# An order of its own for the first head group, and maxima ahead of record turnings in the last tile slot

## What is computed

```python
x = x + attn_a(layernorm(x), w_qkv_a, w_o_a)
x = x + scale * (layernorm(x) @ (2*kernel - 1))
x = x + attn_b(layernorm(x), w_qkv_b, w_o_b)
x = x + scale * (layernorm(x) @ (2*kernel - 1))
# attn: qkv = x @ w_qkv; rope on q and k; four query heads share a key head
# scores = q @ k.T * 0.25, causal; probs = softmax(scores); out = (probs @ v) @ w_o
```

## Time and profile before

| what | value |
|---|---|
| median of 3 runs | 1512.0 us (1511.1 to 1519.8) |
| the profiled execution, its own time | 1511.48 us |
| its span, first to last instruction | 1509.7 us |
| mean granted TensorE clock | 0.949 |

### The profile page before, as it was taken

How to read it: one execution, slowest core, us unless ns; L and a number is a source line. 1 busy time by engine, 2 the same in 40 slices (tenths; PEclk the granted TensorE clock), 3 DMA queues, 4 the chain that set the end, 5 groups by cost and what they waited for, 6 DMA issues and landing times.

```text
span 1509.7 us, 28518 instructions
## 1 busy us (share of the span) xinstructions
PE 1358.1 (90%) x11076; PEld 796.5 (53%) x11076; DVE 1094.9 (73%) x1587; ACT 893.2 (59%) x1704; POOL 384.7 (25%) x591
## 2 busy tenths in 40 slices
PE   5989999999898999999889899999988889999997
PEld 4854444446675444444667544444567744444455
DVE  6667888847767888883776688888376668888647
ACT  3536776773354776775335377777624547777752
POOL 3422222111342222221134222222123412222201
PEclk9988999999897999999999699999999969999999
DMA  3000000001000000000220000000010000000011
GB/s 116 1 1 10 9 16 3 2 2 43 1 1 2 9 16 10 2 3 1 84 70 1 2 9 17 10 2 3 2 41 1 1 1 10 17 9 3 3 51 47
DMA packets 12980, 23.99 MB, mean 16 GB/s; under 512 B 1072, under 2 KB 4144, under 8 KB 12848
## 3 DMA queue, kind: packets, MB, share of 16 engines
q1 hardware_dynamic: 12848, 22.19, 4.3%
HBM read 16.94 MB, written 4.19 MB: 14 GB/s over the span
## 4 chain that ended last, share of the span: by engine, by line
PE 73%; DVE 16%; issue 6%; ACT 3%; POOL 1%; DMA 0%; DVEq 0%; ACTq 0%; POOLq 0%; SPq 0%
PE psO L675 20%; PE psM L539 15%; PE psE L654 14%; PE psM L612 12%; DVE mx L1027 8%; PE psE L592 3%; PE psO L592 3%; PE psM L522 2%; PE psM L619 2%; ACT probs L857 2%; DVE stats L934 1%; PE psM L639 1%; DVE xn L954 1%; DVE attn L1053 1%; PE psE L522 1%
## 5 line engine op out<-in xcount | busy, mean ns | idle before, releaser
L857 ACT ACTIVATE probs<-psE 128x512 f32<-128x512 f32 x1152 | 625.6, 596 | 293.4 <-PE psE L654 287.0
L1027 DVE TENSOR_REDUCE mx<-psM 128x2 f32<-128x768 f32 (+4 forms) x704 | 693.3, 1026 | 121.4 <-PE psM L619 96.3
L612 PE MATMUL psM<-kT,qT 48*128 48x384 f32 (+5 forms) x1536 | 314.5, 423 | 47.4 <-DVE mx L1027 36.6
L675 PE MATMUL psO<-probs,v_grp 128*32 128x512 f32 (+3 forms) x3072 | 324.3, 511 | 0.0
L654 PE MATMUL psE<-qT,kT 50*128 50x512 f32 (+3 forms) x1536 | 293.5, 420 | 15.3 <-ACT probs L857 10.2
L1227 POOL TENSOR_SCALAR_AFFINE_SELECT probs<-probs 128x512 f32<-128x512 f32 x256 | 160.0, 637 | 563.1 <-ACT probs L857 531.0
L612 PEld LDWEIGHTS psM<-kT,qT 48*128 48x128 f32 x1536 | 153.1, 196 | 161.6 <-DVE mx L1027 119.7
L654 PEld LDWEIGHTS psE<-qT,kT 50*128 50x128 f32 x1536 | 134.0, 191 | 171.6 <-ACT probs L857 127.2
L619 PE MATMUL psM<-mask_b 64*128 64x64 bf16 x2048 | 123.9, 201 | 0.0
L675 PEld LDWEIGHTS psO<-probs,v_grp 128*32 128x32 f32 x3072 | 68.4, 110 | 91.1 <-issue 68.5
L539 PE MATMUL psM<-wq_hi,xT_hi 128*128 128x512 f32 (+1 forms) x384 | 98.6, 379 | 9.2 <-ACT vs L823 4.7
(11 more groups left out here) (80 smaller groups left out, 1304.0 us busy)
## 6 DMA issues: line engine op xcount, KB each, us to landing
probs<-in_w_qkv SPq DMA_DIRECT2D x5, 1536.0 KB, 6.5
xs<-in_x SPq DMA_DIRECT2D x8, 512.0 KB, 3.8
xn<-in_w_o SPq DMA_DIRECT2D x16, 256.0 KB, 2.5
out_x<-xs SPq DMA_DIRECT2D x8, 512.0 KB, 2.8
qT<-nm_rows SPq DMA_DIRECT2D x128, 8.0 KB
probs<-in_w_ffn SPq DMA_DIRECT2D x1, 256.0 KB, 8.3
attn<-in_mask SPq DMA_DIRECT2D x1, 160.0 KB, 7.8
sin_s<-in_sin SPq DMA_DIRECT2D x1, 128.0 KB, 8.0
```

Source lines behind the costliest of these rows:

```text
L612: return pe.matmul(psM[:, 2 * pair + h % 2, to:to + k1 - k0], qT[lo:lo + MAXROW, g, qt // QT_PER_CHUNK, h // 2, qt % QT_PER_CHUNK * P:(qt ...
L675: ins = pe.matmul(psO[VW * j:VW * (j + 1), off:off + w], v_grp[:, kb, :], probs[:, (g * NS + s) % PSLOTS, at(j), to:to + w], start=s in (0 ...
L857: act.activation(probs[:, (g * NS + s) % PSLOTS, at(heads[0]):at(heads[0]) + len(heads), 0:w], psE[:, n % SRING, 0:w * len(heads)].rearran ...
L1027: dve.tensor_reduce(to, src, AX.X, ALU.max, negate=True).then_inc(ring_used.sem, 1)
```

## The change

There are three parts. In slot 9, a table of its own puts the two units U.0 and U.1 of tile 6 ahead of the record turnings, and N.0 of group 0 behind R.0 and R.1 (on DVE: behind the copy of R.0). Slot 10 is gone: the units of tile 7 (V.0 to V.3 in the new table) stand in the new `FIRST_ORDER`, the order of group 0 alone, between its first score products. There, Y is `meet(0)`, and the second half of `nm_parts_of(0, ...)` moves on POOL behind the second mask. `FIRST_ORDER` moves N.1.0 and the other entries too. The other groups keep their order. `SLOT_FILL` is not used, and the slices of `cos_s` and `sin_s` are written in another way with the same meaning.

```diff
+FIRST_ORDER = """
+V.0 S.0 V.1 S.1 V.2 S.2 V.3 Y S.3 U.0 PV.0.0 S.4 U.1 PV.1.0 N.1.0 U.2 PV.2.0 OC.0.0 U.3
+S.5 U.4 O.0.0 S.6 U.5 S.7 U.6 U.7 S.8 U.8 PV.3.0 S.9 U.9 U.10 S.10 PV.4.0 U.11 S.11 U.12 S.12 U.13 PV.5.0
...
-PE_SLOT = "TX U.0 Q.0 R.0 R.1 U.1 Q.1 R.2 U.2 R.3 Q.2 R.4 U.3 R.5 Q.3"
...
-SLOTS_A = range(-4, TILES + 4)
-SLOT_NM = TILES + 1
+SLOT_FILL, SLOT_LAST = 2, TILES + 1
+PE_SLOT = {None: "TX U.0 Q.0 R.0 R.1 U.1 Q.1 R.2 U.2 R.3 Q.2 R.4 U.3 R.5 Q.3"}
...
+PE_SLOT[SLOT_LAST] = "U.0 U.1 R.0 R.1 N U.2 R.2 R.3 U.3 R.4 R.5"
+DVE_SLOT[SLOT_LAST] = "U.0 U.1 RC.0 N U.2 RC.3 U.3"
+SLOTS_A = range(-4, TILES + 2)
...
-    return [w for w in words(GROUP_ORDER) if has_prev or len(w) < 3 or w[2] >= 0]
+    return words(GROUP_ORDER if has_prev else FIRST_ORDER)
...
                     for s in DIAGONAL:
                         mask(g, s)
+                        if g == 0 and s == DIAGONAL[1]:
+                            nm_parts_of(0, 1)
...
                 nm_parts_of(0, 0)
-                nm_parts_of(0, 1)
                 group(0, True)
```

More of the change, by code:

```diff
@@ L216 @@
        "RC": 2, "ST": -4, "RS": -3, "AP": -2}
-PE_SLOT = "TX U.0 Q.0 R.0 R.1 U.1 Q.1 R.2 U.2 R.3 Q.2 R.4 U.3 R.5 Q.3"
-ACT_SLOT = "HI RC.1 RC.2 RS PH RC.4 RC.5 QC"
-DVE_SLOT = "AP COS U.0 RC.0 LO ROPE U.1 RC.3 U.2 ST U.3"
-SLOTS_A = range(-4, TILES + 4)
-SLOT_NM = TILES + 1
+SLOT_FILL, SLOT_LAST = 2, TILES + 1
+PE_SLOT = {None: "TX U.0 Q.0 R.0 R.1 U.1 Q.1 R.2 U.2 R.3 Q.2 R.4 U.3 R.5 Q.3"}
+ACT_SLOT = {None: "HI RC.1 RC.2 RS PH RC.4 RC.5 QC"}
+DVE_SLOT = {None: "AP COS U.0 RC.0 LO ROPE U.1 RC.3 U.2 ST U.3"}
+PE_SLOT[SLOT_LAST] = "U.0 U.1 R.0 R.1 N U.2 R.2 R.3 U.3 R.4 R.5"
+DVE_SLOT[SLOT_LAST] = "U.0 U.1 RC.0 N U.2 RC.3 U.3"
+SLOTS_A = range(-4, TILES + 2)
 def slot_work(text, n):
     out = []
-    for what, *arg in words(text):
+    for what, *arg in words(text.get(n, text[None])):
+        if what == "N":
+            out.append((what, arg, 0))
+            continue
         t = n - LAG[what]
@@ L257, in ring_jobs @@
     for n in SLOTS_A:
-        if n == SLOT_NM:
-            out.append((("N", 0, 0), None))
-        out += [(("U", 0, units_of(t)[arg[0]]), unit_pair(units_of(t)[arg[0]])) for what, arg, t in slot_work(PE_SLOT, n) if what == "U"]
+        for what, arg, t in slot_work(PE_SLOT, n):
+            if what == "N":
+                out.append((("N", 0, 0), None))
+            elif what == "U":
+                out.append((("U", 0, units_of(t)[arg[0]]), unit_pair(units_of(t)[arg[0]])))
     turn = 0
@@ L263, in ring_jobs @@
         for what, *arg in group_order(g > 0, g < KV - 1):
-            if what in ("U", "N", "O"):
-                out.append(((what, g + 1, arg[0]) if what == "U" else (what, g + arg[1], arg[0]), turn % 2))
+            if what in ("U", "V", "N", "O"):
+                job = ("U", 0, units_of(TILES - 1)[arg[0]]) if what == "V" else ("U", g + 1, arg[0]) if what == "U" else (what, g + arg[1], arg[0])
+                out.append((job, turn % 2))
                 turn += 1
@@ L732, in group @@
                             tiles[what](arg[0], arg[0] % 2)
+                        elif what == "V":
+                            unit(0, units_of(TILES - 1)[arg[0]])
                         elif what == "U":
@@ L744, in round_ @@
                 for n in SLOTS_A:
-                    if n == SLOT_NM:
-                        nm_turn(0, 0)
                     for what, arg, t in slot_work(PE_SLOT, n):
-                        if what == "TX" and t > 0:
+                        if what == "N":
+                            nm_turn(0, 0)
+                        elif what == "TX" and t > 0:
                             turn_xn(r, t, t % 2)
@@ L882, in group @@
                             o_copy(g + arg[1], arg[0])
-                        else:
+                        elif what not in ("X", "Y", "V", "U", "N"):
                             other(what, arg[0] if arg else None)
@@ L1058, in group @@
                     for what, *arg in group_order(has_prev, has_next):
-                        if what == "U":
+                        if what == "V":
+                            unit(0, units_of(TILES - 1)[arg[0]])
+                        elif what == "U":
                             unit(g + 1, arg[0])
-                        elif what == "X":
-                            meet(g + 1)
+                        elif what in ("X", "Y"):
+                            meet(g + 1 if what == "X" else 0)
                         elif what == "N":
@@ L1068, in round_ @@
                 for n in SLOTS_A:
-                    if n == SLOT_NM:
-                        nm_copy(0, 0)
                     for what, arg, t in slot_work(DVE_SLOT, n):
-                        if what == "LO" and t > 0:
+                        if what == "N":
+                            nm_copy(0, 0)
+                        elif what == "LO" and t > 0:
                             lo(r, t, psE[:, t % 2, :])
@@ L1085, in round_ @@
                             ln_a(r, t)
-                meet(0)
                 group(0, False, True)
@@ L1171, in rope_sin @@
                     t4 = t_s[:, k].rearrange("p (h a d) -> p h a d", a=2, d=HALF)
-                    sn = sin_s[:, bass.ds(l, 1), t, :]
+                    sn = sin_s[:, l:l + 1, t, :]
                     for a in range(2):
```

4 lines of the change are left out of this document (3 added, 1 removed).

## The result

The changed kernel is slower: 1551.41 us, median of 4 executions, beside 1515.9 for the kernel before, ratio 1.020 (95% interval 1.014 to 1.027). 1487 had been forecast. Executions of one and the same kernel scatter here, those of the kernel before from 1509 to 1575 (66 of them, 19 above 1530), and the ratios leave out the ones far above their kernel's fastest. What the scatter is turned out to be half of the answer.

A forecast was written before the change was run, and what follows sets the result against it. TensorE, 90% busy, was taken to set the pace, the changed stretch costing mostly low clock. Gains of 30.6 us from 1511.48 gave 1480.9; 6.0 us of clock falls made 1487, own range 1480 to 1496.

The forecast's parts named there:

- Slot 9: From where TensorE ran dry to V.0: 7.8 us, where it was 11.45 in round 1 and 9.99 in round 2.
- rival two: Clock stays down in group 0 as before, only slot 9 gains 13.1 us: time 1498, chance 0.19.
- The waits up to S.5: Group 0, V.0 at 101.65 to S.5 at 113.0: TensorE idle about 1.7 us for N.1's rows, transfer 2.4.
- sum at full clock: Slot 9 through group 0: 7.8 + 31.35 = 39.1 us per round, gaining 30.6 us in four rounds, so 1480.9.
- 18 maxima, then fully loaded: Group 0 from S.5: VectorE fully loaded with 18 maxima, 17.8 us, 20.0 with copy, division and gaps.
- the clock: Before S.5 the clock may fall: 0.65 per round, 1.5 falls of 1.54 us each, 6.0 us over four rounds.
- the clock stays down as before: Same as rival two: group 0 stays at low clock, only slot 9 gains; 1498, chance 0.19.
- The fall behind S.5: Clock fall from the thin stretch U.2, PV.2, U.3 and 1.7 us idle before S.5; given 0.65 per round.
- what follows S.5 is dense, so I count 1.5 such falls: Group 0 after S.5: dense work limits the cost to 1.5 falls of 1.54 us each time.
- The slower rival: Low clock over the whole stretch from V.0 on, 52.9 us per round: time 1536, chance 0.05.
- The rule on short idle moments: Short idle moments between matmul groups suffice to swing the clock; in group 0 that would give nearer to 1498.
- The 1498 that was derived from it: Total time in us if the clock went on swinging in group 0, only slot 9 gaining 13.1.

The follow-up runs named there:

- slot9_heads: Kernel before with slot 9's new order alone, plus three unread full-width products in the heads of groups 0 to 6: 1501.27 us, ratio 0.992.
- before_heads: Kernel before, with three unread full-width products in the wait before U.5 of groups 0 to 6: 1514.4 us.
- slot9_full2: slot9_full with two products in place of three in the head of a group: 1479.62 us, ratio 0.978.
- after_full2: Changed kernel with full-width products, two in the heads of groups 1 to 6, others before U.0, V.0 and S.1 to S.5: 1516.43 us, ratio 0.995.
- fill_all: fill_first and one more repeated pair before U.5 in each of groups 1 to 6: 1512.0 us, ratio 1.002.
- slot9_only: Slot 9's new order alone, the rest from the kernel before: 1530.57 us, ratio 1.008.
- after_again: The changed kernel unaltered, a second set of six executions: 1536.39 us beside 1514.55 for the kernel before, ratio 1.015.
- fill_first: Changed kernel with unread pairs of 48-row products: two before U.0, two before V.0, three before S.5: 1514.65 us, ratio 1.000.
- first_order_only: The new FIRST_ORDER alone, slot 9 as in the kernel before: 1578.86 us, ratio 1.033.
- slot9_full: slot9_heads with full-width products also in thin spots of slot 9, tile 7 and group 0 (before U.1 and N.1): 1486.71 us, ratio 0.983.

## Why the prediction was wrong

**Slot 9 was right.** 7.8 us had been worked out, 7.29 were measured, with V.0 at 101.21 for 101.65. slot9_heads against before_heads gives 13.1 us between the medians (of two sets), for the 13 that rival two had named as slot 9's gain. This is all that the change gives.

**The waits up to S.5 were right.** S.5 came at 114.57 for 113.0, with 6.8 us of low clock in front of it that the 113.0 had left out, and an idle spell of 1.33 us for 1.7; the transfer took 2.6 us from the copy's end to S.5 for 2.4. At full clock V.0 to S.5 is 7.90 + 3.26 = 11.2 us, for 11.35.

**The step "sum at full clock" failed in what it compared.** 39.1 us per round was set against 47.28 as if the difference were the order's. Beyond slot 9's part it was the clock's: the old group 0 behind the new slot 9 takes 39.3 at full clock with its fillers (slot9_full2), the new one about 40.2 without them (from after_full2 and fill_all). So the 4.5 us per round that 31.35 for 35.83 had promised were not there to be had from the order: against the old one at full clock the new one costs 0.9 us or more. The term of the sum that was too small is "18 maxima, then fully loaded": 20.0 us from S.5 to group 1, and 21.7 measured to the cut (482.22 to 503.95 in after_full2). There TensorE waited for VectorE five times and for ScalarE three times, and VectorE was not fully loaded but stood idle for 4.0 us waiting for TensorE, which one sum per engine doesn't see. The last 0.8 of it is in group 1's head: its first score product indeed doesn't wait for the last maximum, but its second unit does.

**The step "the clock" failed by size.** It counted 0.65 x 1.5 falls per round of 3.5 us each, some 14 us of low clock in four rounds. Summed from the stretches' mean clocks it is about 102 us in the first profile of the changed kernel and 73 in the second; before it was 88. The stretches, forecast at 4 x 39.1 + 6.0 = 162 us, took 198.0 and 187.0. One fall like that of rows 8 had been taken as the measure. But the rows 2 showed another kind as well, the 17 us one, and the rival that rested on it ("the clock stays down as before") was given 0.19. It was the right one for the stretch and still too mild. The fall behind S.5, for which 0.65 had been given, is the one that lasts: with the wait before S.5 filled, the median drops by 19 us. The fall among V.0 to V.3, in each round of both profiles, had not been expected at all. No run fills those spots alone, so what it costs is not shown. The sentence "what follows S.5 is dense, so I count 1.5 such falls" is the one that was wrong.

**The step that was missing: groups 1 to 7.** The prediction held them fixed at 27.9. They depend on the stretch through the clock. Shown: a caught group loses 2.8 us, up to six follow one another, and filling the heads ends this in both kernels; in the kernel before it ends most of the scatter too. Each such round costs 15 to 17 us. These groups make up 34.8 us of the loss in the first profile and 24.5 in the second. The slower rival, priced at 1536 with low clock inside the stretch alone, came near the size by luck: most of the loss (34.8 of 47.3 us, 24.5 of 26.1) lay where it had put none.

Not shown: why some rounds are caught and others not. How close in front of group 1 the clock comes back doesn't decide it: in the changed kernel this is within a us of the cut in rounds 1 and 3, and only round 3 is caught. Nor is the old group 0 safe. In slot9_only the clock comes back 16.8, 16.6 and 16.9 us ahead of group 1 in rounds 1, 2 and 4, which are caught, and 17.7 us ahead in round 3, which is not; in the kernel before it is 17.2 to 18.0, and no round is caught. Three of these eight, in this order slot9_only's rounds 1 and 3 and round 1 of before:

```profile
121.50:138.30 16.80, 15.84 (x147) 6.79 (x143) 13.84 (x16) 13.22 (x25) 2.88 (x6) 1.00 0.06 18
886.08:903.79 17.71, 16.76 (x163) 7.25 (x155) 14.02 (x17) 13.45 (x26) 2.88 (x6) 1.00 0.05 17
```

```profile
123.83:141.16 17.33, 16.38 (x153) 7.04 (x145) 13.82 (x16) 13.21 (x25) 2.90 (x6) 1.00 0.05 17
```

So in these eight rounds a few tenths of a us, from the end of the last fall to group 1, separate the caught from the others. The equal rounds of two executions fit with that: where the last fall ends seems to set where the later ones come. What would try it is a pure shift of group 1 without other edits, and that wasn't run. One fall in a head is not enough for all that follow either: in four rounds (of slot9_only, after_again, fill_first and first_order_only) the series broke off after three to five groups. Why a fall lasts 6.8 us here and 27 there also stays open.

The rule on short idle moments that the prediction cited from the Trainium skill (page "TensorE: Matmul & The Clock Gate", section "A second HAM failure mode: psum-queue depth-cycling") is borne out: no wait in a group's head is over 0.67 us, and in rounds 3 and 4 the clock swings once per group. (The "under 1 us" that the prediction gave for the trace before is just missed: the wait from 106.14 to 107.15, 1.01 us, spans the start of the 17.07 us fall.) The 1498 that was derived from it was too low in both places: by 24 us in the stretches of the first profile, 198.0 for 174, and by 35 in the groups behind.

## What to carry to other kernels

Where a profile shows TensorE busy for 90% and a mean clock under 1, sum the low clock by stage before pricing any reordering. A stretch that is long because its clock is low is not long because of its order, and its time at full clock must be had first, by filling its idle spots for one run. Short waits among narrow products are worth filling with full-width products that nobody reads, two to six at a time (0.7 to 1.7 us in the traces): slot9_full2 is 22 us below slot9_heads and 33 below the kernel before at the same output, and its four executions lie within 2 us. A filler that stands behind a wait lengthens the kernel: the five before S.1 to S.4 cost 1.7 us per round. And before a change is judged on three executions, look at the granted clock of each.

## What the runs showed that I had not expected

- Falls of 6.8 us recur at the same place in a loop of 27.93 us, up to six groups in a row: five at 30.7 to 31.0 us and a sixth, which takes 27.0 without a fall, at 29.8. This is in the traces of slot9_only and of the changed kernel. The kernel before reached 1575 us at a mean clock of 0.90, probably by the same, but no such execution was profiled.
- Pairs of 48-row products in the same wait of a head (fill_all) did not prevent the fall, full-width ones did, though the engine was busy for nearly as long (26.87 us in a group of fill_all, 27.02 in one of slot9_full2). Whether it is the height or these 0.15 us was not separated.
- Two full-width products in a head are as good as three and cost next to nothing: groups of 27.98 us, for 28.22 with three and 27.93 with none, and 7 us between slot9_full and slot9_full2.
